# Two gather tiles moved from GpSimd's indirect DMA to row-by-row DMAs on ScalarE's queue

## The reference

```python
h = relu(layernorm(x))                                   # per node
w = (silu(silu(edge_attr_8 @ W1 + b1) @ W2 + b2)) @ W3 + b3   # 256 weights per edge
m = messages(h[src], edge_attr_4, w)                     # 32 values per edge
out = x + h_self(h; Ws, Wv) + segment_sum(m, dst, 100000) / 4
```

## Time and profile before

| | us |
|---|---|
| median of 3 runs | 610.87 (608.48 to 611.92) |
| the profiled execution | 610.19 |
| its span, first to last instruction | 608.4 |
| POOL busy in the span | 486.0 |
| PE busy | 522.6 |
| DVE busy | 412.1 |
| ACT busy | 405.7 |

### The profile page before, as it was taken

One profiled execution on the slowest core, in us unless ns is written; L12 is line 12 of the kernel. 1 busy time (PEld: TensorE's weight loads), 2 busy tenths in 40 slices (PEclk: granted clock), 3 DMA queues, 4 the chain that ended last, 5 costly groups with the idle time before them and its releaser, 6 DMA issues.

```text
span 608.4 us, 13260 instructions
## 1 busy us (share of the span) xinstructions
PE 522.6 (86%) x3255; PEld 414.2 (68%) x3255; DVE 412.1 (68%) x1142; ACT 405.7 (67%) x1215; POOL 486.0 (80%) x391
## 2 busy tenths in 40 slices
PE   5877988888978797599999899999899999959790
PEld 4776777776865674577777677776676777736590
DVE  5686777777785775477787767777777587643820
ACT  3433555454556785589998888988888698847430
POOL 6777777777777777888888888888888888888777
PEclk9968999998988787587888788889886778866555
DMA  4654765655641111222222222222222222222222
GB/s 129 190 157 123 196 171 173 182 169 153 193 122 15 14 15 14 10 10 11 11 10 10 12 11 9 12 10 11 12 9 11 10 12 10 11 10 10 8 10 9
DMA packets 54262, 34.40 MB, mean 57 GB/s; under 512 B 37830, under 2 KB 41656, under 8 KB 54200
## 3 DMA queue, kind: packets, MB, share of 16 engines
q0 software_dynamic: 34176, 6.28, 20.2%
q1 hardware_dynamic: 12854, 14.63, 8.3%
q10 hardware_dynamic: 7170, 12.81, 5.7%
HBM read 17.59 MB, written 16.08 MB: 55 GB/s over the span
## 4 chain that ended last, share of the span: by engine, by line
SPq 62%; issue 16%; PE 8%; DVE 5%; DMA 4%; POOL 3%; ACT 1%; ACTq 0%; DVEq 0%
SPq L292 44%; SPq L288 12%; DMA xin<-in_x_dram 4%; POOL out_dram L332 3%; PE ps L713 2%; SPq L225 1%; SPq L275 1%; PE ps L616 1%; DVE oc L856 1%; DVE ps L848 1%; PE ps L586 1%; PE ps L610 1%; DVE ps L821 1%; PE ps L601 1%; PE ps L716 1%
## 5 line engine op out<-in xcount | busy, mean ns | idle before, releaser
L332 POOL DMA_INDIRECT out_dram<-sums,idx_i x196 | 306.3, 1563 | 62.0 <-issue 57.1
L319 POOL DMA_INDIRECT xg<-in_x_dram,src_all x186 | 178.8, 961 | 57.7 <-issue 56.4
L713 PE MATMUL ps<-msg,eq 128*128 128x32 f32 (+1 forms) x980 | 140.1, 295 | 13.1 <-DVE carry L993 11.2
L713 PEld LDWEIGHTS ps<-msg,eq 128*128 128x128 f32 x980 | 136.1, 217 | 14.0 <-DVE carry L993 11.6
L1017 DVE TENSOR_TENSOR prod<-ps,coef 128x256 f32<-128x256 f32 (+1 forms) x245 | 98.7, 470 | 16.6 <-PE ps L662 14.3
L486 ACT ACTIVATE dsq<-ps,dcol 128x512 f32<-128x512 f32 x196 | 87.7, 546 | 0.2 <-PE ps L675 0.2
L662 PE MATMUL ps<-w3blk,x 64*128 64x256 f32 x392 | 73.9, 509 | 0.0
L509 ACT ACTIVATE eq<-dsq,onecol 128x384 f32<-128x384 f32 x147 | 73.8, 528 | 0.0
L472 ACT ACTIVATE sums<-ps 128x132 f32<-128x132 f32 x49 | 13.7, 280 | 87.4 <-PE ps L716 64.5
L384 ACT ACTIVATE sqT<-ps 128x512 f32<-128x512 f32 (+2 forms) x50 | 29.3, 585 | 63.7 <-PE ps L601 63.4
L662 PEld LDWEIGHTS ps<-w3blk,x 64*128 64x128 f32 x392 | 44.6, 248 | 36.8 <-issue 31.8
(11 more groups left out here) (106 smaller groups left out, 832.6 us busy)
## 6 DMA issues: line engine op xcount, KB each, us to landing
xg<-in_x_dram SPq DMA_DIRECT2D x1192, 0.1 KB
xin<-in_x_dram SPq DMA_DIRECT2D x48, 256.0 KB, 2.8
out_dram<-oc ACTq DMA_DIRECT2D x48, 256.0 KB, 2.5
out_dram<-sums,idx_i POOLq DMA_INDIRECT x196, 3.1
xg<-in_x_dram,src_all POOLq DMA_INDIRECT x186, 2.5
er_all<-in_edge_attr_dram SPq DMA_DIRECT2D x1, 780.0 KB
sh_all<-in_edge_attr_dram SPq DMA_DIRECT2D x1, 390.0 KB
xin<-in_x_dram SPq DMA_DIRECT2D x1, 192.0 KB
```

The source lines that it names most:

```text
L319: pool.indirect_dma_start(xg[:, t * D:(t + 1) * D], None, x, bass.IndirectOffsetOnAxis(ap=src_all[:, t:t + 1], axis=0)).then_inc(signal, 16)
L332: pool.indirect_dma_start(out, bass.IndirectOffsetOnAxis(ap=idx_i[:, k % NS, a:a + 1], axis=0), sums[:, k % NS, a * DR:a * DR + D], None, ...
L713: m = pe.matmul(psSUM[:, a * DR:a * DR + n], eq[:, k % 2, o:o + P], msg[:, k % 2, b, 0:n], start=(b == a), stop=(not carried and (b == a - ...
```

## The change

SP keeps its ten tiles of 1192 rows (186 to 195). POOL gathers 184 tiles in place of 186. Tiles 184 and 185, 256 rows, are gathered row by row on ACT's queue, by a `gather_rows` of its own: six rows behind the store in each of the steps 12 to 47 (216 rows), then 20 rows in each half of the first edge pass. The late units keep their tiles; the second one now waits for ACT's rows too. `row_i` and `row_at` hold twelve tiles and not ten, so SP loads two more pieces of `row_i`. ACT's loop over the steps 8 to 47 is written out.

```diff
-    GT, RT = 10, 10
+    GT, RT, RA = 10, 12, 2
     G1 = T + 1 - RT
+    G2 = G1 + RA
...
-    LATE_UNITS = [range(GF, GF + 30), range(GF + 30, G1), range(G1, T + 1)]
+    LATE_UNITS = [range(GF, GF + 30), range(GF + 30, G2), range(G2, T + 1)]
...
-            late_rows = iter([(t, p) for t in range(G1, T + 1) for p in range(P if t < T else TAIL)])
+            late_rows = iter([(t, p) for t in range(G2, T + 1) for p in range(P if t < T else TAIL)])
...
+            rows_of_tiles = iter([(t, p) for t in range(G1, G2) for p in range(P)])
+            offsets = []
+
+            def gather_rows(count):
+
+                for t, p in itertools.islice(rows_of_tiles, count):
+                    if p % 32 == 0:
+                        o = (t - G1) * P + p
+                        _, offsets[:] = nc.values_load_multi_w_load_instructions(
+                            row_at[0:1, o:o + 32], engines=[mybir.EngineType.Activation], min_val=0, max_val=(N - 1) * D * 4,
+                            skip_runtime_bounds_check_because="src holds rows of x")
+                    act.dma_start(xg[p:p + 1, t * D:(t + 1) * D].bitcast(u8), x_bytes[:, ds(offsets[p % 32], D * 4)])\
+                       .then_inc(gathered_row[t - G1], 16)
...
-            with act.Fori(1, DLOOP) as i:
-                for k in range(DBODY):
-                    node_step(i * DBODY + k, k + DBODY, i)
-            for c in range(FULL, NCH + 2):
-                node_step(c, c, DLOOP)
+            for c in range(DBODY, NCH + 2):
+                node_step(c, c, min(c // DBODY, DLOOP))
+                if c == 12:
+                    act.wait_ge(s["rows_at"], 2)
+                if 12 <= c < FULL:
+                    gather_rows(6)
...
+                    if first:
+                        gather_rows(P * RA - 6 * (FULL - 12) - 20 if h else 20)
```

More of the change, by code:

```diff
@@ L211, in rows @@
             return ap[ds(r0, p * r), :].rearrange("(p r) d -> p (r d)", p=p), p, r * D
+        x_bytes = x.bitcast(u8).rearrange("n d -> (n d)").rearrange("(a n) -> a n", a=1)
         block = ctx.enter_context(nc.Block(no_gpsimd_drain=True))
@@ L276, in _ @@
             sp.dma_start(out[N:N + BT * P, :].rearrange("(p r) d -> p (r d)", p=P), spare0[:, :]).then_inc(s["spare_stored"], 16)
-            x_bytes = x.bitcast(u8).rearrange("n d -> (n d)").rearrange("(a n) -> a n", a=1)
-            late_rows = iter([(t, p) for t in range(G1, T + 1) for p in range(P if t < T else TAIL)])
+            late_rows = iter([(t, p) for t in range(G2, T + 1) for p in range(P if t < T else TAIL)])
             nodes = []
@@ L1059, in late_landed @@
                 if tiles[0] < G1:
-                    dve.wait_ge(gathered_late[n - EARLY], 16 * len(tiles))
-                else:
-                    for t in tiles:
+                    dve.wait_ge(gathered_late[n - EARLY], 16 * len([t for t in tiles if t < G1]))
+                for t in tiles:
+                    if t >= G1:
                         dve.wait_ge(gathered_row[t - G1], 16 * (P if t < T else TAIL))
```

## The result

The changed kernel is slower. Its runs beside the kernel before took 636.1 us in the median (627.3 to 640.2) against 610.2; the ratio is **1.030, 95% interval 1.025 to 1.036**. The prediction was 622.8 us with a range of 611 to 632 and "slower" as the likeliest sign.

The account below looks back on a forecast made before the run. SP's queue was taken to bound the kernel, the last chunk load's issue fixing the end. ACT's delay as SP feels it, with 1.3 us of fetches included, gave 610.19 + 12.6 = 622.8 us, other terms 0; range 611 to 632, likeliest 616 to 630.

Parts of the forecast that it names:

- What bounds the kernel: Whole kernel: SP's last row sets the end, fixed by when the last chunk load is issued; POOL is 2.2 us behind.
- Two gathers less, worth 0: POOL before its first scatter: two gathers cost 2.52 us, but DVE's indices hold the late scatters, so 0 on the path.
- Two more fetches, +1.3 us: SP ahead of the loads of chunks 8 to 12: two row-number fetches move node stage and SP's rows by +1.3 us.
- Six rows behind each store: ACT's node stage: six rows take 1.93 us; steps 13 to 42 take 114.7 us with loads, against 97.6 before.
- add in full: ACT's steps: every 32 rows a load of addresses, 2.6 us each, lengthens its step in full; five loads, 13.0 us.
- From ACT's delay to SP's: Load of chunk 49: ACT falls back 17 us, slack swallows part; SP's last load, last row and the end come 12.6 us later.
- Forty rows in the first edge pass: ACT after the node stage: 15.4 us more; POOL waits up to 12 us, at most +7, hidden behind SP's 12.6.
- rival 2: Edge stage: SP's delay is small, but POOL stands idle behind the first edge groups; 617 us; chance 0.08.
- Rival 1: Node stage: ACT's rows fit into its idle time, only SP's 1.3 us of fetches show; 611.5 us; chance 0.20.
- Rival 3: POOL is what counts: SP's last row at least 4.7 us earlier wins the waits and two gathers; 605.5 us; chance 0.05.
- Rival 4: Dearer rows: two queues disturb each other, 0.05 us more for each of 180 rows; 632 us; chance 0.07.
- The two rules: Skill rules: issue usually small relative to the DMA, giving 611.5 us, disputed by the trace; ScalarE's queue of 8, favouring Rival 1.

Follow-up runs that it names:

- the stalled chips: Two other chips used for the last four runs, where every kernel, the one before too, took about 845 us because of a stall in the first 280 us.

## Why the prediction was right in its sign and short in its size

The profiled execution took 628.8 us where 622.8 were forecast. By the two lines worked out above, 4.9 of these 6.0 us are SP's (17.5 and not 12.6), and the last 1.1 are POOL's, which passed SP's line.

**What bounds the kernel, right.** SP's last row set the end before, with POOL 2.2 us behind. Making the addresses earlier moved SP by 3.0 us and the time by no more than POOL's slack; taking two gathers from POOL gave nothing.

**Two gathers less, worth 0: right.** The run without rows on ACT shows it. The price of 1.26 us a gather shows only where SP's line is not the last. The prediction took the 2.5 us off POOL's line, as it should; since that line ended last in the changed kernel, they counted there.

**Two more fetches, +1.3 us: right for the loads, short for the rows.** The loads of chunks 8 to 12 moved from 32.05 to 33.39, 1.34 us. DVE's conversion of the addresses in the kernel before, then SP's loads and DVE's conversion in the changed one:

```profile
45.30 0.80 DVE L949 TENSOR_SCALAR row_at<-row_i 1x1280 int32<-1x1280 int32 x1
```

```profile
33.39 3.01 SPq L229 DMA_DIRECT2D xin<-in_x_dram  x5
```

```profile
47.10 1.16 DVE L969 TENSOR_SCALAR row_at<-row_i 1x1536 int32<-1x1536 int32 x1
```

The conversion moved by 1.80 us and takes 0.36 longer, and SP's first row moved by 2.1; what was left out of the sum as "some tenths" is 0.46 us by which the conversion came later still and 0.36 by which it is longer, more than half of the term. The run without rows on ACT has 2.7 us at SP's last row, but at the last pair of loads only 2.06 (166.99 against 164.93), so its node stage adds nothing to the 2.1 of the first row. The other 0.6 us come in the 940 rows behind it, when ACT's written-out loop is over: from the load of chunk 49 to the last row it is 374.1 us and not 373.5, and between 373.5 and 374.6 in all kernels but those of the stalled chips. On the stalled chips, too, the written-out loop shows nothing: SP's rows took 489.8 us with it alone and 489.6 to 490.7 with the loop kept.

**Six rows behind each store: the sum was close, in part by luck.** ACT's row took a median of 0.235 us and a pitch of 0.32 (1.93 us for six), the even steps without a load 3.24 us, the odd ones 3.28 to 3.44 (3.4 and 3.7 were forecast). A load of addresses takes 2.42 us (2.6 forecast). For the 30 steps the model gave 114.7 us, and the changed kernel had 117.3; without the loads it gave 101.7, and the run with one load had 104.4. But the difference of 2.6 us is the net of two larger ones.

Six steps without a load are too long: steps 18, 30, 31, 34 and 35 of the changed kernel took 4.3 to 4.6 us and step 36 5.7, 27.9 us in all where the model has 20.4. In them PE's granted clock was between 0.5 and 0.71, and an odd step at the lower level takes 4.32 us with six rows or with none (step 31 here and in the kernel without rows on ACT). The other 24 steps are 4.9 us under the model. Of this 2.9 us are steps 23, 29 and 39, each behind an even step with a load: they took 2.62 to 2.67 us. The prediction had a load "add in full", which holds in the odd steps alone.

So a term for PE's clock was missing, up to 7.5 us here, and the rest of the model was too dear. The prediction took the even step's 3.24 us, PE's way from the copy to the centred chunk, from one row at the full clock. ACT's rows are not shown to be what lowers the clock. The kernel without them has a mean of 0.91 in the same stretch, the one with the edge rows only 0.91, the one with the addresses made earlier 0.90. The kernel before, with 0.98, is the exception, in one execution. What the traces show the rows to change is what a low clock costs: where SP paces the stage, ACT's and PE's waits for it take it up, and where ACT and PE pace it, the stage gets longer. The two kernels whose ACT programs are the same up to there took 117.3 us for the 30 steps at 0.87 and 122.8 at 0.78. One profile of each stands behind this pair, and no run was made that changes the clock alone; how much lower the clock is because of the rows stays open.

**From ACT's delay to SP's: right.** The load of chunk 49 came 181.6 - 178.20 = 3.4 us after step 43 began (3.6 forecast). It stands at 181.6, not 178.0: 1.2 us from the later start of step 13 (60.94 against 58.44, where 1.3 was allowed), 2.6 from the steps, less 0.2. Of the 17.5 us at SP's last row, 16.3 are there at this load. The remaining 1.2 us came in the 374 us of rows behind it, without a cause that the trace names; that stretch differs by as much between the kernels.

**Forty rows in the first edge pass, "hidden behind SP, POOL at most +7": wrong.** This is the step that failed in its mechanism, though in time the larger miss is SP's 4.9 us. Group 3's indices came at 273.42, 3.3 us over its bound of 270.1. But the larger fault is that it looked for POOL's wait at group 3 alone. There, POOL had 27.8 us of room: it would reach the group at 258.3, and its indices of before were made at 230.58. The later groups had less. DVE's indices of groups 6 and 10 in the kernel before, then in the changed one:

```profile
269.86 0.15 DVE L1007 TENSOR_TENSOR idx_i<-idx_f,trash 128x4 int32<-128x4 f32 x1
...
297.11 0.15 DVE L1007 TENSOR_TENSOR idx_i<-idx_f,trash 128x4 int32<-128x4 f32 x1
```

```profile
301.47 0.15 DVE L1027 TENSOR_TENSOR idx_i<-idx_f,trash 128x4 int32<-128x4 f32 x1
...
334.19 0.15 DVE L1027 TENSOR_TENSOR idx_i<-idx_f,trash 128x4 int32<-128x4 f32 x1
```

POOL would reach group 6 at 235.97 + 6 x 7.46 = 280.7 us, only 10.9 us after its indices of before, and group 10 at 310.6, 13.5 after. The indices came 31.6 and 37.1 us later. So POOL had lost 21.2 us by group 6 and 24.0 by group 10, where the prediction had 12. (At group 4 it had lost 19.3 of them, 285.11 against 265.8.) Its line was a span of 627.8 us and not the 615.5 that go with the 617 us of rival 2, level with SP's. Rival 2 ("the first edge groups hold POOL") was thus no rival but a second mechanism beside the first, and priced at less than half: 7.1 us over the kernel before, where POOL's line was 19.4 over it. In time it cost little, some 1 us, since SP's line was at 625.9 anyway. Taking the forty rows away gained nothing: POOL lost 10.7 us there before 300 us and not 24, and SP's line, later by the clock, set the end.

**The rivals.** Rival 1 (the rows fit into ACT's idle time) fell for the change as it is, but it holds in part: six rows in even steps fit entirely, six rows in odd steps cost 1 us a step, most of which SP's slack takes: with one load of addresses the 30 steps are 7.7 us longer than without rows on ACT, and SP's last row 2.5 later. That kernel, all 256 rows in it, is at 614.0 us, where rival 1 had 611.5. What does not fit are the loads. Rival 3 (POOL is what counts) had 605.5 us for a lead of SP of at least 4.7 us and two gathers. The kernel that has a lead of 5.1 us and one gather took 607.2; by the same sum, 610.19 - 2.2 - 1.26 = 606.7. Against the runs of the kernel before that stand beside it (609.5) it won 2.3 us of these 3.5. Rival 4 (dearer rows) fell: ACT's rows take 0.235 us, SP's 0.228 as before.

**The two rules.** The Trainium skill, DMA: Bandwidth & Descriptors, section "Issuing engines are not separate DMA queues", calls the time to issue a DMA usually small relative to the DMA itself. For one row of the kernel before the trace agrees: the last one was issued at 538.8, and DVE, which waited for it, went on at 540.37, 1.55 us later against 0.32 for the issue. It does not follow that the issue is free. A new row is issued every 0.32 us while those before it are still under way, so the issues add up and the transfers do not, and the kernel before ends by SP's 1192nd. The prediction's "the trace disagrees" is right of the sum of the rows and not of one row.

The Trainium skill, Advanced Engine Details and Errata, section "Engine Queue Depths", gives ScalarE a queue of 8. The trace shows DMAs issued beside arithmetic, not how deep the queue is: in the even steps rows were issued while the squares and the rectifier ran (128.92 and 129.24 in the timeline of the kernel with one load), and in step 29, an odd one, two of six came ahead of the root (122.32). In steps 27 and 31 all six came last. The copy, which stands behind all six rows and sometimes a load, still had to wait for their issue, 28.6 us in 14 waits.

## What to carry to other kernels

An in-order engine that also computes can take over DMA issues only in the steps in which another engine sets its pace: here six rows in an even step cost nothing and six in an odd one a microsecond. Count the register loads of a DMA with a dynamic address as DMAs of their own, since one of them here takes as long as seven rows, and look for a place where the engine waits anyway: in an odd step a load added 2.8 us, in an even one half of that. Before an engine is relieved, name the line that ends last and the one behind it: with SP's last row 5.1 us earlier, one gather less on POOL was worth its full 1.3 us, and with nothing moved on SP two gathers less were worth nothing. When a sum comes out close, check its steps one by one: here 7.5 us too little and 4.9 too much stood in it. And where a whole stage shifts, check the consumer's room at each of its steps, not at the one whose row is at hand.

## What the runs showed of the hardware that was not expected

PE's granted clock in the node stage was 0.98 in the kernel before, 0.89 to 0.91 in six others on the same chip (the one without rows on ACT among them), 0.87 in the changed kernel and 0.78 in the one with the node rows only. It was low not only where PE waits for ACT: in the kernel without rows on ACT it fell after PE had waited 3.3 us for DVE, in the changed kernel in steps 18, 30, 31 and 34 to 36, where ACT sets the pace. An even step of 3.24 us at the full clock then took 4.4 to 5.7 us, an odd one up to 4.32. Where SP paces the stage this did no harm: the 30 steps took 96.7 us at a mean of 0.91 and 97.6 at 0.98. Where PE is on the path it makes the stage longer.

ACT's load of 32 addresses takes 2.42 us, SP's 2.12. ACT issues some of its DMAs beside its own arithmetic, three of six rows in the even step shown, two in step 29 and none in steps 27 and 31, so the place of a DMA in the program is not by itself its place in time.
